# One core, a long-convolution and a 4-bit feed-forward layer: DMA transposes of the first output half, sizes on ScalarE, earlier chunk products, low part first

## The reference

```python
dt = exp(log_dt); A = -exp(log_A_real) + 1j * A_imag; dtA = A * dt[:, None]
Cs = Cc * (exp(dtA) - 1.0) / A
K = 2.0 * einsum('hn,hnl->hl', Cs, exp(dtA[:, :, None] * arange(1024))).real
y = irfft(rfft(x * mask) * rfft(K)) + x * mask * D[:, None]      # then masked again
w[k, n] = q[k, n] * s[g, n] - (z[g, n] + 1) * s[g, n]            # g = k // 128
gate = y @ Wg; up = y @ Wu                                       # 1024 -> 2752
out = x + ((gate * sigmoid(gate) * up) @ Wd).astype(float16)     # 2752 -> 1024
```

## Time and profile before

| | us |
|---|---|
| median of 3 runs | 1173.37 (1173.34 to 1173.43) |
| profiled execution | 1176.32 |
| its span in the trace | 1174.4 |
| TensorE busy | 1149.5 |
| VectorE busy | 887.7 |
| ScalarE busy | 847.5 |
| GpSimd busy | 222.0 |

### The profile page before, as it was taken

How to read it: one execution, slowest core, us unless ns; L and a number is a source line. 1 busy time by engine, 2 the same in 40 slices (tenths; PEclk the granted TensorE clock), 3 DMA queues, 4 the chain that set the end, 5 groups by cost and what they waited for, 6 DMA issues and landing times.

```text
span 1174.4 us, 15087 instructions
## 1 busy us (share of the span) xinstructions
PE 1149.5 (98%) x5562; PEld 954.5 (81%) x5562; DVE 887.7 (76%) x985; ACT 847.5 (72%) x1398; POOL 222.0 (19%) x139
## 2 busy tenths in 40 slices
PE   5999999999999999999999999999999999999996
PEld 5999998788888888888888888888888888888883
DVE  7678745677777777777777988887777777777775
ACT  6443204887888788788788797777888887888873
POOL 0122000211422422211111252111211211211213
PEclk8999999999999999999999999999999999999999
DMA  7878778441653556434434875455344334444514
GB/s 282 283 229 254 238 263 222 111 108 27 159 138 99 150 147 178 109 87 121 115 81 118 261 186 143 152 180 160 91 108 120 96 108 111 105 108 108 152 53 163
DMA packets 66976, 173.94 MB, mean 148 GB/s; under 512 B 11654, under 2 KB 17222, under 8 KB 66902
## 3 DMA queue, kind: packets, MB, share of 16 engines
q1 hardware_dynamic: 64834, 171.14, 50.7%
q10 hardware_dynamic: 2036, 1.81, 0.5%
q0 software_dynamic: 32, 0.03, 0.0%
HBM read 159.94 MB, written 15.83 MB: 150 GB/s over the span
## 4 chain that ended last, share of the span: by engine, by line
PE 94%; DMA 2%; DVE 2%; issue 1%; POOL 0%; ACT 0%; SPq 0%; DVEq 0%; POOLq 0%
PE pair L1257 28%; PE pair L1298 27%; PE pair L1278 27%; PE pair L1211 11%; DMA toep<-kernel_padded 1%; PE pair L1170 1%; PE pair L1191 0%; DMA kernel_padded<-k_sb 0%; POOL o L590 0%; PE pair L1327 0%; PE pair L1360 0%; DMA logs<-in_L_cond_log_dt_dram 0%; PE pair L1347 0%; PE pair L1338 0%; DVEq L175 0%
## 5 line engine op out<-in xcount | busy, mean ns | idle before, releaser
L1023 DVE SCALAR_TENSOR_TENSOR acc<-pair,s_down,acc 128x1024 f32<-128x1024 f32 x328 | 420.3, 1283 | 189.7 <-PE pair L1298 189.3
L703 ACT ACTIVATE pair<-pair,ratio 128x512 f32<-128x512 f32 x616 | 382.3, 665 | 101.4 <-PE pair L1257 101.2
L722 ACT ACTIVATE pair<-pair,ratio 128x512 f32<-128x512 f32 x581 | 360.7, 659 | 117.8 <-PE pair L1278 117.7
L1257 PE MATMUL pair<-high,wg 128*128 128x512 f32 x704 | 278.6, 396 | 0.0
L1257 PE MATMUL pair<-low,wg 128*128 128x512 f32 x704 | 277.1, 394 | 0.0
L1298 PE MATMUL pair<-mid_h,wd 128*128 128x512 f32 x688 | 268.2, 392 | 0.0
L1298 PE MATMUL pair<-mid_l,wd 128*128 128x512 f32 x672 | 265.7, 395 | 0.0
L1278 PE MATMUL pair<-high,wu 128*128 128x512 f32 x672 | 265.0, 394 | 0.0
L1278 PE MATMUL pair<-low,wu 128*128 128x512 f32 x672 | 264.0, 393 | 0.0
L542 POOL CAST mid_h<-sil 128x1024 fp32r<-128x1024 f32 (+1 forms) x43 | 45.2, 1052 | 694.5 <-DVE sil L1000 684.0
L1257 PEld LDWEIGHTS pair<-high,wg 128*128 128x128 f32 x704 | 132.1, 188 | 31.3 <-ACT pair L703 1.1
(11 more groups left out here) (150 smaller groups left out, 589.9 us busy)
## 6 DMA issues: line engine op xcount, KB each, us to landing
q_in<-rows_backwards SPq DMA_DIRECT2D x86, 512.0 KB, 4.6
z_in<-zeros_plus_one SPq DMA_DIRECT2D x130, 256.0 KB, 4.7
toep<-kernel_padded SPq DMA_DIRECT2D x64, 512.0 KB, 6.7
q_in<-_L_ffn_down_qweight_dram SPq DMA_DIRECT2D x42, 512.0 KB, 4.8
u_all<-in_x_dram SPq DMA_DIRECT2D x13, 512.0 KB, 10.9
x_fin<-in_x_dram SPq DMA_DIRECT2D x12, 512.0 KB, 9.3
out_dram<-x_fin SPq DMA_DIRECT2D x12, 512.0 KB, 5.6
high_parts<-staged SPq DMA_DIRECT2D x8, 512.0 KB, 2.9
```

The costliest lines, as they stand in the source:

```text
L703: act.activation(gate_ps[:, tb, :], gate_ps[:, tb, :], ACT.Copy, scale=ratio[:, 0, G * t + g:G * t + g + 1]).then_inc(gate_scaled, 1)
L722: act.activation(up_ps(tau)[:, tb, :], up_ps(tau)[:, tb, :], ACT.Copy, scale=ratio[:, 1, G * t + g:G * t + g + 1]).then_inc(up_scaled, 1)
L1023: dve.scalar_tensor_tensor(out=acc[:, hid, :], in0=ps, scalar=scale, in1=acc[:, hid, :], op0=ALU.mult, op1=ALU.add).then_inc(down_taken, 1)
L1257: mm = pe.matmul(gate_ps[:, tb, :], w["g"][tau % 2][:, g, :], rows[:, g, 512 * tb:512 * tb + 512], start=g == 0 and part == 0, stop=part = ...
```

## The change

There are six edits. Names are those of the code.

1. `sizes` for the chunks 0 and 1 leave VectorE: ScalarE makes them with eight activations of 128 x 64 (Exp with the parameter as scale), and it loads its Exp table for them before. VectorE copies only the first parameter out of PSUM, makes the angles of chunk 0 straight from PSUM, and then copies the rest.
2. The order of transposes is changed around that: half of `turn(5)` goes behind the first product on TensorE, and ScalarE takes one half of group 3 before and one behind `angles(0)`.
3. The products of the chunks 3 to 8 are multiplied in front of part `hh` = 1 of `convolve(g + 2)` instead of part 3.
4. `load_toeplitz(g + 2)` on SP goes ahead of the first weight loads, where both are in iteration g = 12.
5. `turn_out` goes from TensorE. SP issues 32 DMA transposes instead (`turn_and_store`), four in each of the iterations tau = 25 to 32, into a new SBUF tile `turned`, and `finish` becomes one addition of two SBUF operands in step 1 and one in step 3 of every second tile. The `down` blocks now alternate between their two PSUM pairs without a shift.
6. In the first half each pair of matmuls takes `low_1` before `high`.

The diff, cut to its core:

```diff
+def down_at(tau, hid):
+    return NH * tau + hid
...
         def parts_of(tau):
-            return high, (low_2 if tau >= NT else low_1)
+            return (high, low_2) if tau >= NT else (low_1, high)
...
                     store_kernels(chunk_begun_at(g - 2))
+                load_toeplitz(g + 2)
                 if g == NG - 4:
...
                     load_weights("u", 0)
-                load_toeplitz(g + 2)
...
+            def turn_and_store(v):
+                j, part = divmod(v, 2)
+                if v == 0:
+                    sp.wait_ge(o16_done, NH)
+                elif part == 0:
+                    sp.wait_ge(out_ready, 2 * j)
+                    for tt in (2 * j - 2, 2 * j - 1):
+                        store_out(0, tt)
+                if j < 4:
+                    for hid in range(4 * part, 4 * part + 4):
+                        sp.dma_start_transpose(turned[:, :, P * hid:P * hid + P], o16[:, hid, 2 * P * j:2 * P * j + 2 * P]
+                                               ).then_inc(rows_turned, 16)
+                if part and j in (1, 2):
+                    for tt in (2 * j + 2, 2 * j + 3):
+                        sp.wait_ge(out_stored[tt % 4], 16)
+                        load_x(0, tt)
...
-            take_rows(0, 3)
-            sizes(1, 0, 8)
-            act.activation(warm[:], ident[:, 0:1], ACT.Sin)
-            take_rows(3, 4)
+            take_rows(1, 3)
+            act.activation(warm[:, 1:2], ident[:, 0:1], ACT.Exp)
+            act.wait_ge(par_copied, 1)
+            for h in range(8):
+                act.activation(size[:, h, :], tab[:, C_B:C_B + 64], ACT.Exp, scale=par[:, 0, h:h + 1]
+                               ).then_inc(first_sizes, 1)
+            act.activation(warm[:, 0:1], ident[:, 0:1], ACT.Sin)
+            take_turned(3, 0)
             angles(0)
+            take_turned(3, 1)
...
-            do(dve.tensor_copy(par[:], par_ps[:, 0:4 * H].rearrange("p (v h) -> p v h", v=4)))
+            dve.tensor_copy(par[:, 0], par_ps[:, 0:H]).then_inc(par_copied, 1)
+            theta_0 = bass.AP(par_ps.tensor, par_ps.offset + H, [par_ps.ap[0], [1, 4], [0, 64]])
+            do(dve.tensor_tensor(theta[:, 0:4], theta_0, bass.AP(tab[:].tensor, C_B, [[C_N, P], [0, 4], [1, 64]]), ALU.mult))
+            dve.tensor_copy(par[:, 1:4], par_ps[:, H:4 * H].rearrange("p (v h) -> p v h", v=3)).then_inc(par_copied, 1)
...
-            exp_sizes(0, 0, 8)
-            turn_angles(0)
...
+            def finish(tt):
+                dve.wait_ge(rows_turned, 16 * NH * (tt // 2 + 1))
+                dve.wait_ge(x_fin_in[tt % 4], 16 * (tt // 4 + 1))
+                to = x_slot(0, tt)
+                dve.tensor_tensor(to, turned[:, tt % 2], to, ALU.add).then_inc(out_ready, 1)
...
-                    if hh == 3 and chunk_begun_at(g - 2) is not None:
+                    if hh == 1 and chunk_begun_at(g - 2) is not None:
                         multiply_kernel(chunk_begun_at(g - 2))
...
-            def turn_out(j):
-                at = turn_at(j)
...
-                pe.wait_ge(down_taken, at - 1)
-                for i in range(2):
-                    to = down_ps[at % 2][:, i, :].bitcast(F16)
-                    for hid in range(NH):
-                        mm = pe.transpose(to[:, P * hid:P * hid + P],
-                                          o16[:, hid, P * (2 * j + i):P * (2 * j + i) + P], ident16[:])
-                mm.then_inc(down_mm, 1)
```

More of the change, by code:

```diff
@@ L41 @@
 QRING = 4
-TURN_AT, TURN_STEP = 181, 8
+TURN_FROM = NT + 3
 SPLIT_FROM = 4
@@ L260, in build_program @@
         staged = sb("staged", [P, HALF], F32R)
+        turned = sb("turned", [P, 2, HID], F16)
         ai_loaded, c_loaded, d_loaded = sem("ai_loaded"), sem("c_loaded"), sem("d_loaded")
@@ L487, in _ @@
                         load_x(0, tt)
[L488 to L497, removed]
+                if TURN_FROM <= tau <= TURN_FROM + HALF_G:
+                    turn_and_store(tau - TURN_FROM)
             for tt in range(4):
@@ L644, in _ @@
             take_rows(8, HEAD_TURNS)
-            sizes(2, *place_of(2))
+            sizes(1, *place_of(2))
             angles(2)
@@ L890, in combine @@
                 a, b = arg[:, here, 32:64], cosine[:, here]
-                dve.wait_ge(sizes_done, max(c, 1))
+                if c < 2:
+                    dve.wait_ge(first_sizes, 4 * c + 4)
+                else:
+                    dve.wait_ge(sizes_done, c - 1)
                 dve.wait_ge(angles_done, 2 * c + 2)
@@ L1117, in _ @@
                         center("d", TAIL)
-                    if TURN_AT <= n < TURN_AT + 4 * TURN_STEP and (n - TURN_AT) % TURN_STEP == 0:
-                        finish((n - TURN_AT) // TURN_STEP)
+                    if g in (1, 3) and tau > TURN_FROM and (tau - TURN_FROM) % 2 and tau < TURN_FROM + HALF_G:
+                        finish(tau - TURN_FROM - 1 + g // 2)
                     if tau == 0:
@@ L1160, in _, with turn @@
             pe.wait_ge(ident_in_sb, 16)
-            def turn(g):
+            def turn(g, halves=(0, 1)):
                 pe.wait_ge(x_loaded[g], 16)
-                for k in range(2):
+                for k in halves:
                     n = 2 * g + k
@@ L1180, in _ @@
             mm.then_inc(par_turned, 1)
-            for g in range(3, 6):
+            for g in range(3, 5):
                 turn(g)
+            turn(5, (0,))
             def multiply_kernel(c):
@@ L1228, in _ @@
             multiply_kernel(0)
+            turn(5, (1,))
             for g in range(6, HEAD_TURNS):
@@ L1336, in rows_second @@
                 taken_before(NH)
+                if tt == 0:
+                    pe.wait_ge(ident16_ready, 1)
                 for hid in range(NH):
@@ L1374, in _ @@
                             down(n // NH, n % NH)
-                    if TURN_AT <= n < TURN_AT + 4 * TURN_STEP and (n - TURN_AT) % TURN_STEP == 0:
-                        turn_out((n - TURN_AT) // TURN_STEP)
                     if not is_tail(tau):
```

27 lines of the change are left out of this document (9 added, 18 removed).

## The result

| | before | after |
|---|---|---|
| median of 6 runs each, us | 1173.4 (1172.89 to 1178.68) | 1188.61 (1185.35 to 1190.2) |
| ratio, 95% interval | | 1.0119 (1.0097 to 1.0141) |
| span of the profiled execution, us | 1174.4 | 1187.4 |
| mean granted clock | 0.995 | 0.986 |

What follows compares the result with a forecast made beforehand. TensorE, busy 98% of the span, was taken as the bound. +11.5 (waits) + 4.8 (clock) - 2.0 (tile) - 3.5 (transposes) + 0 + 0 = +10.8 us on the 1173.4 median gave 1184.2 us, range 1176 to 1191.

Steps and rivals of the forecast that it cites:

- Edit 3: Convolution: products two parts sooner make TensorE wait for VectorE's joins of chunks 5 to 8, +11.5 us in sum.
- Rival D: Convolution: VectorE's joins run ahead once products come sooner, so the products don't wait; 1167.9 us, chance 0.07.
- The port pair: Chunk 5's and 6's chains: VectorE operations held by GpSimd's subtraction keep their 2.46 us instead of 0.42, three times.
- Rival C: Convolution: the port lock is lost, chunk 5 loses 4.0 us of its wait and chunk 6 2.0; 1175.0 us, chance 0.08.
- The clock: TensorE behind the three waits of 2.9 to 4.3 us: a clock fall each, 1.6 us apiece, +4.8, bounds 0 to 8.4.
- rival B: Convolution: the waits come without a fall of the clock, or at most one; 1179.4 us, chance 0.20.
- Edit 4: Convolution, group 14: the tile ahead of the weights removes the 1.96 us wait at 171 us, -2.0 us.
- Edit 5: Second half: TensorE loses four transposing blocks, -3.5 us; DMA transposes and `finish` on VectorE cost 0.
- rival E: Second half: late DMA transposes make `finish` hold VectorE and through it the `down` blocks; 1216 us, chance 0.04.
- Edit 6: First half of the feed-forward stage: low part first, same matmuls, taken as 0, bounds 2.2 us either way.
- Rival F: First half: the swapped matmul order sets the pace, 2.2 us either way; 1182.0 or 1186.4 us, chance 0.06.
- Edits 1 and 2: Start: a shorter VectorE list to the first join and four moved TensorE transposes cancel, 0, bounds -0.7 and +0.4 us.

Runs made afterwards that it cites:

- experiment 2: The kernel before with edit 3 alone (products in front of part 1 instead of part 3): 1190.67 us, ratio 1.0137.
- experiment 8: The kernel after, with GpSimd's subtractions of groups 4, 5 and 7 held back until VectorE ended the operation they used to meet: 1181.26 us, ratio 1.0062.
- experiment 6: The kernel before with edit 6 alone (low part first in the first half): 1174.11 us, ratio 1.0005.
- experiment 3: The kernel after, with 36, 22 and 28 unused transposes on TensorE before the products of groups 6, 8 and 10: 1178.45 us, ratio 1.0047.
- experiment 7: The kernel before with edit 4 alone (shifted kernel tile loaded ahead of the first weights): 1172.38 us, ratio 0.9986.
- experiment 9: Two runs: the kernel before with edits 4, 5 and 6, 1169.1 us (0.9942); the kernel after without edit 3, repeated, 1169.01 us (0.9946).
- experiment 10: The kernel after, unchanged, run again for a second profile: 1186.96 us, ratio 1.0112 against the kernel before.
- experiment 5: The kernel before with edit 5 alone (output transposes by DMA, `turn_out` gone): 1168.27 us, ratio 0.9956.
- experiment 1: The kernel after without edit 3 (products behind the third part again): 1170.63 us, ratio 0.9953.
- experiment 4: The kernel after with the products moved one part sooner instead of two: 1176.32 us, ratio 1.0019.

## Why the prediction was right

**Edit 3.** The steps held: chunk 5, 6, 7 and 8 were forecast to make TensorE wait 4.3, 2.9, 3.5 and 0.8 us and do so 4.31, 2.85, 3.44 and 0.83 us. What made them readable is that the joins hang on the end of the group before and not on the product. The chunks 3 and 4 were taken as 0 within 0 to 0.5; chunk 3 waits 1.05 (0.62 in the second profile), so this bound was too narrow. Part of that wait only takes the place of a tile wait just before it: the two together are 0.7 to 1.05 us in all five profiles with the products in front of part 1. Rival D is out by experiment 2.

**The port pair.** Kept, as forecast: the 2.4 us operations are there in after, at 86.11, 98.26 and (for chunk 6) 123.89, and its second profile has them too. Rival C was a real possibility: experiment 8 breaks the overlaps, and the waits fall by 2.0 and 2.0. The Trainium skill has the rule (SBUF — State Buffer, the section "SBUF: two separate sides"): of the two engines the one that starts second is held for the whole instruction of the other. The trace agrees where VectorE starts second: the join, and `z_one` as much, ends 0.2 to 0.3 us behind the subtraction. A long hold of GpSimd by VectorE isn't in these rows; its subtraction takes 2.54 us where it starts inside a VectorE operation of 0.42 (at 97.88), and 2.35 to 2.42 elsewhere. Rival C priced the gain of chunk 5 at 4.0, though; it is 2.0, since the first subtraction finds another operation of the same chain to hold up.

**The clock.** The mechanism was right and the size too small: three falls at 1.6 us each (4.8) were 6.6, inside the bounds of 0 to 8.4. The value was taken from one of two rows at the start, 1.6, and not from 2.8; the falls measured in full work run from 1.4 to 3.0, and 2.2, the middle of the two rows, is the mean of the three. That there would be exactly three was partly luck: after had three in both its profiles, but in experiment 2 the same 2.85 us wait brought none. The prediction also judged by length: it set the three waits against the 1.96 us one behind which the clock had stayed, and experiment 6 has the fall behind 1.94 us at that very place. Experiment 3 shows that the falls come from the idle time, and rival B (1179.4) is out for this kernel.

**Edit 4.** Right: the 1.96 us wait goes (experiment 7) and the weights are late for nobody: TensorE goes from the convolution into the first gate block without a wait.

**Edit 5.** Right on TensorE: -3.5 forecast, -3.5 between the traces. The DMA transposes cost nothing, and rival E is out. They are no free issue, though: four hold SP's queue for 5.1 to 8.0 us, and with a median landing of 3.1 the first addition has some 3 us left (766.93 + 3.1 to 773.25), and next to nothing with the longest, 6.2, where the prediction counted 13 in all. The Trainium skill gives 1.309 us for a square of 128 x 128 (VectorE: DVE Perf Modes, The three transpose paths). By that figure the prediction estimated 10.5 us for eight squares. They took less here: the four DMAs, of two squares each, held SP for 5.1 us at best (1.25 each in the median), and with a landing of 3.1 that makes at most some 8. The other page says that transposing DMAs are as fast as ordinary ones (Advanced Engine Details and Errata, X-Bar Transpose (TRN2)). For the landing the trace doesn't contradict it: 3.1 us for 64 KB, beside 3.0 for an ordinary 32 KB in the earlier trace rows. The issue is slower: an ordinary one took 0.59 in the row.

**Edit 6.** Right: no change of pace, in experiment 6 and in the trace of after. Rival F is out.

**Edits 1 and 2.** Taken as 0 within -0.7 and +0.4: the first convolution starts 0.5 later in this profile and a wait of 0.36 behind it is gone. Experiment 9 leaves their worth open.

**The sum.** +10.8 was forecast for the span and +13.0 measured. The 2.2 between them are the clock (+1.8), chunk 3's wait (+1.05), the start (+0.5), the tile wait at 51 us that went (-0.4) and 0.7 less at the end: +2.3, to the precision of such readings. Some luck is in that closeness: the profile of before and this one of after both ran most of their second half at the slower of two paces (below), which no term of the sum knew of. The second profile of after ran at the faster one, and its span of 1182.5 is only 8.1 above before's. The medians differ by 15.2 in the first comparison and by 12.3 in experiment 10. The prediction also took "within 0.1 us" from three runs; the runs of one kernel spread by 2 to 9 us here (1170.26 to 1178.98 for before in the largest set).

## What to carry to other kernels

Before an operation is moved ahead on the engine that bounds a kernel, lay the end of its producer beside the new arrival, from the event that starts the producer; here that gave four waits to 0.1 us. The clock's falls can't be foreseen one by one in this way: give them a mean and bounds. An early arrival at an in-order engine gains nothing where nobody waits for the result, and its wait is paid twice, since TensorE's clock can fall behind it; where such a wait can't be avoided, work that nobody reads can keep the clock up, as in experiment 3. Ship the edits apart: one of six hid a gain of half a per cent.

## What the runs showed of the hardware

**A matmul stream with two paces.** The feed-forward stage of the same code runs at one of two steady paces, at a granted clock of 1.00 in both. The first instruction of one `up` block and that of the block 84 steps later, in after, and then in the second profile of the same kernel:

```profile
846.73 0.40 PE L1289 MATMUL pair<-high,wu 128*128 128x512 f32 x1
1079.69 0.40 PE L1289 MATMUL pair<-high,wu 128*128 128x512 f32 x1
```
```profile
844.92 0.40 PE L1289 MATMUL pair<-high,wu 128*128 128x512 f32 x1
1075.64 0.40 PE L1289 MATMUL pair<-high,wu 128*128 128x512 f32 x1
```

232.96 / 84 is 2.773 us a step and 230.72 / 84 is 2.747. Over the second half's 160 steps that is 4.3 us, 0.37% of the kernel. In the kernels whose output is transposed by DMA one pace holds for the whole second half: the faster in the profiles of experiments 3, 5, 8 and 10, the slower in after's first and in those of experiments 1, 4 and 9. In the kernels with the four transposing blocks the pace changes at the blocks: before's steps are 2.746 to 2.748 between the first and second block and between the third and fourth, and 2.773 elsewhere; experiments 2, 6 and 7 change too, and behind the fourth block 2 and 6 are slow and 7 fast. So a disturbance of the stream can change the pace, which then holds to the next one. In the first half the two paces are 2.787 and 2.780 (experiment 1's kernel had the one in its first profile and the other in its second). No edit picks the pace; what does is open. The two profiles of after differ by 4.9 us in span, and the pace explains 4.2 of them. For runs without a profile that isn't shown. The lesson for readers: a difference of 4 us between two profiles must first be looked for in this step.

**The clock's fall hangs on more than the wait's length.** Waits of 1.64 (experiment 9), 1.94 (6), 2.02, 2.85, 3.44 and 4.31 us were followed by a granted clock of 0.50; waits of 1.57 (experiment 5), 1.96 (before), 2.32 and, in another kernel, again 2.85 were not. The 1.94 and the 1.96 are the same wait in the same code. A fall costs 1.4 to 3.0 us of full work; the same wait of 2.85 us cost 1.4 in one profile of after and 2.9 in the other. What decides is open.

**What the prediction read at the start was weak evidence.** The same stretch at the start in after and then in experiment 3 (the eighth column is the clock):

```profile
15.20:18.00 2.80, 2.80 (x16) 2.68 (x15) 2.32 (x7) 2.19 (x9) 0.00 (x0) 0.50 1.03 417
```
```profile
15.20:18.00 2.80, 2.80 (x15) 2.68 (x14) 2.29 (x7) 2.67 (x11) 0.00 (x0) 1.00 1.03 417
```

The record says 0.50 and 1.00, but the 16 transposes there take 3.68 and 3.62 us, the same slow pace (8 take 0.91 at full clock). So at this place the record of the clock and the lengths of known instructions disagree, and the lengths are what the time is made of.
